# Landmark attention and group norms on one core: five moved or reshaped steps in the second stage, and shorter chains for three norms

## What is computed

```python
x = x + proj(softmax(q.T k) v)           # first stage: group norm (8 groups, weight and bias), 8 heads
u = group_norm(x, 32 groups)             # no weight, no bias
x = x + conv3(dwconvs(u)) * u            # depth-wise convolutions in bands
t = tokens(x)                            # 1024 tokens of 128 channels an image
n = layer_norm(t)                        # second stage
q, k, v = n Wqkv + bqkv                  # 8 heads of 16, landmarks: every 64th token, 16 of them
K1 = softmax(q k_lm.T); K2 = softmax(q_lm k_lm.T); K3 = softmax(q_lm k.T)
z = newton_inverse(K2, 6 steps)          # z = 2 z - z K2 z
t = t + (K1 (z (K3 v))) Wproj + bproj
g = softmax(layer_norm(t) Wg); top 2 of 8 experts, their weights normalised
t = t + sum_e score_e (gelu(n W1_e + b1_e) W2_e + b2_e)
t = t + dense_attention(layer_norm(t))   # third stage
t = t + gated_silu_experts(layer_norm(t))  # top 6 of 16, with two shared experts
```

## Time and profile before

| | us |
|---|---|
| median of 3 runs | 5484.53 |
| lowest and highest run | 5480.68 and 5505.98 |
| the profiled execution | 5477.94 |
| its span in the profile | 5476.1 |
| PE busy | 4820.5 (88%) |
| DVE busy | 3578.8 (65%) |
| ACT busy | 2948.8 (54%) |
| POOL busy | 1017.9 (19%) |
| mean granted clock of PE | 0.953 |

### The profile page before, as it was taken

The page is one execution under the profiler, slowest core; times in us unless marked ns, Lnnn a source line. Parts: engine busy times, 40 slices in busy tenths (PEclk is TensorE's granted clock), DMA queues, the critical chain, the costliest instruction groups (busy, mean ns, idle before and its releaser), DMA issues.

```text
span 5476.1 us, 81744 instructions
## 1 busy us (share of the span) xinstructions
PE 4820.5 (88%) x25601; PEld 2609.5 (48%) x25601; DVE 3578.8 (65%) x7699; ACT 2948.8 (54%) x5390; POOL 1017.9 (19%) x1348
## 2 busy tenths in 40 slices
PE   5888888888888886967999899999899999999999
PEld 1222222222222221335888888888755555555554
DVE  6677777777776772646666666665676766766765
ACT  2555566555655654423555555556655455555552
POOL 2211211121212212211434334343200000000000
PEclk7999999999999998987999999999999999999999
DMA  2522222222222221222555455554311111111112
GB/s 85 147 71 71 76 89 71 71 71 71 71 83 71 72 74 32 30 68 83 154 165 173 140 176 154 164 170 116 109 49 46 52 46 48 51 43 52 51 46 74
DMA packets 406296, 477.08 MB, mean 87 GB/s; under 512 B 87640, under 2 KB 249648, under 8 KB 403760
## 3 DMA queue, kind: packets, MB, share of 16 engines
q1 hardware_dynamic: 372128, 424.84, 25.5%
q0 software_dynamic: 20576, 35.55, 2.4%
q10 hardware_dynamic: 13168, 11.48, 0.8%
HBM read 308.54 MB, written 145.57 MB: 83 GB/s over the span
## 4 chain that ended last, share of the span: by engine, by line
PE 30%; DVE 12%; issue 4%; ACT 4%; DVEq 3%; POOL 2%; DMA 1%; ACTq 0%; SPq 0%; POOLq 0%
PE n_ps_f L2155 4%; PE n_ps_f L2148 4%; PE n_ps_xy L1803 3%; PE n_ps_h L1793 3%; PE n_ps_c L2195 2%; PE n_ps_h L2207 2%; POOL rows_scratch L1313 2%; PE n_ps_f L2142 2%; PE n_ps_f L1654 1%; PE n_ps_xy L2211 1%; PE n_ps_h L2211 1%; DVEq L2027 1%; DVE n_down_weights L2026 1%; PE n_ps_f L995 1%; ACT n_hidden L1609 1%
## 5 line engine op out<-in xcount | busy, mean ns | idle before, releaser
L597 ACT ACTIVATE a_probs<-ps_b 128x512 f32<-128x512 f32 x2048 | 1110.7, 594 | 800.4 <-PE ps_b L693 787.5
L454 DVE TENSOR_REDUCE a_negmax<-ps_a 128x1 f32<-128x1024 f32 x1024 | 1206.4, 1219 | 384.5 <-PE ps_a L637 374.8
L637 PE MATMUL ps_a<-a_k_stack,a_q_stack 96*128 96x512 bf16 x2048 | 635.6, 397 | 181.4 <-DVE a_negmax L454 89.8
L693 PE MATMUL ps_b<-a_q_stack,a_k_stack 99*128 99x512 bf16 x2048 | 675.0, 392 | 67.5 <-ACT a_probs L597 30.6
L1609 ACT ACTIVATE n_hidden<-n_ps_h,n_b 128x128 f32<-128x128 f32 x1472 | 420.4, 374 | 402.6 <-PE n_ps_h L1793 399.1
L706 PE MATMUL ps_o<-a_probs,a_v_ones 128*32 128x512 f32 x4096 | 561.8, 621 | 0.2 <-ACT a_probs L597 0.2
L637 PEld LDWEIGHTS ps_a<-a_k_stack,a_q_stack 96*128 96x128 bf16 x2048 | 146.3, 99 | 736.4 <-DVE a_negmax L454 470.2
L1803 PE MATMUL n_ps_xy<-n_down_weights,n_hidden 128*128 x2944 | 402.6, 280 | 56.1 <-ACT n_hidden L1609 30.2
L693 PEld LDWEIGHTS ps_b<-a_q_stack,a_k_stack 99*128 99x128 bf16 x2048 | 196.7, 100 | 486.4 <-ACT a_probs L597 247.0
L1803 PEld LDWEIGHTS n_ps_xy<-n_down_weights,n_hidden 128*128 128x128 f32 x2944 | 363.4, 193 | 86.7 <-issue 83.1
L2092 ACT ACTIVATE n_down_weights<-n_ps_h 128x512 f32<-128x512 f32 x288 | 172.4, 599 | 427.7 <-PE n_ps_h L2207 318.5
(11 more groups left out here) (350 smaller groups left out, 7485.5 us busy)
## 6 DMA issues: line engine op xcount, KB each, us to landing
n_up_weights<-in_L_ffn_W_dram SPq DMA_DIRECT2D x368, 256.0 KB
n_up_weights<-score_scratch SPq DMA_DIRECT2D x512, 128.0 KB, 2.9
split_scratch<-a_pieces SPq DMA_DIRECT2D x180, 256.0 KB
a_q_stack<-split_scratch SPq DMA_DIRECT2D x128, 192.0 KB, 3.4
a_k_stack<-split_scratch SPq DMA_DIRECT2D x128, 192.0 KB, 4.0
rows_scratch<-n_zero SPq DMA_DIRECT2D x16, 1472.0 KB
outs_scratch<-n_xy SPq DMA_DIRECT2D x176, 128.0 KB
n_xg<-rows_scratch SPq DMA_DIRECT2D x80, 256.0 KB, 4.7
```

Source lines behind the costliest of these rows:

```text
L454: dve.tensor_reduce(negmax[:, b, t:t + 1], bank, axis=AX.X, op=ALU.max, negate=True).then_inc(ring_read, 1)
L597: act.activation(probs[:, m % PROBS, 512 * k:512 * k + 512], ps_b[:, k, :], ACT.Exp).then_inc(b_exp, 1)
L637: last = pe.matmul(bank[:, cols], q_stack[0:KS, h, 128 * t:128 * t + 128], k_stack[0:KS, h, cols], start=True, stop=True)
L693: pe.matmul(ps_b[:, k, :], k_stack[:, h, 128 * t:128 * t + 128], q_stack[:, h, 512 * k:512 * k + 512], start=True, stop=True).then_inc(b_u ...
```

## The change

In the second stage:

- *Landmarks.* `k_lm` is written from the projection's PSUM bank with the bias added in the same instruction, as soon as PE has written it, and not from `kt`. ACT's `kt` (which used to be what the landmarks waited for) now waits for `lm_up`, and PE's K3 product at slot 19 gets a wait for `kt` of its own.
- *Bias.* PE's second bias product moves from slot 36 to 39, DVE's second addition from 38 to 40.
- *Norm.* The choice's layer norm yields to slot 4 at n == 3, one step later.
- *Key weights.* The sums over the landmark weights (L1406) move from behind the first Newton step to ahead of the Newton loop; the reciprocal stays where it was.
- *Exponential.* ACT's exponential of the choice moves from slot 14 to 17, DVE's part of the choice behind it from 16 to 18.

In the norms:

- `rsqrt` has ten instructions instead of eleven: the multiplication by -0.5 goes into the middle instruction of each Newton step.
- `group_affine` becomes `group_scale` with `rsqrt_column`: the variance is formed as minus one half of itself, and each Newton step takes two instructions instead of three, with a column as the scalar operand. The shift is no longer part of it: "norm" forms it in one instruction with weight and bias, "norm2" in one of its own, and the second norm's scale and shift are written where the later stage reads them, without the copies.

```diff
 def rsqrt(dve, y, v, t):
     dve.tensor_scalar(y.bitcast(I32), v.bitcast(I32), -0.5, 1597463007.0, ALU.mult, ALU.add)
-    dve.drain()
-    dve.tensor_scalar(v, v, -0.5, None, ALU.mult)
     for _ in range(3):
         dve.drain()
         dve.tensor_tensor(t, y, y, ALU.mult)
         dve.drain()
-        dve.tensor_tensor(t, t, v, ALU.mult)
+        dve.scalar_tensor_tensor(t, t, -0.5, v, ALU.mult, ALU.mult)
...
+def rsqrt_column(dve, out, y, minus_half, t):
+    dve.tensor_scalar(y.bitcast(I32), minus_half.bitcast(I32), -0.5, 519526879.0, ALU.mult, ALU.add)
+    dve.drain()
+    for n in range(3):
+        dve.scalar_tensor_tensor(t, y, minus_half, y, ALU.mult, ALU.mult)
+        dve.drain()
+        dve.scalar_tensor_tensor(out if n == 2 else y, t, 1.5, y, ALU.add, ALU.mult)
+        dve.drain()
...
-def group_affine(dve, scale, shift, group, sums, sums_read, width, small, eps):
+def group_scale(dve, scale, group, sums, sums_read, width, small, eps):
...
-    dve.tensor_tensor(small[:, 0:1], group[:, 0:1], group[:, 0:1], ALU.mult)
+    dve.scalar_tensor_tensor(small[:, 0:1], group[:, 0:1], 0.5, group[:, 0:1], ALU.mult, ALU.mult)
...
-    dve.tensor_tensor(small[:, 1:2], group[:, 1:2], small[:, 0:1], ALU.subtract)
+    dve.scalar_tensor_tensor(small[:, 1:2], group[:, 1:2], -0.5, small[:, 0:1], ALU.mult, ALU.add)
...
-    dve.tensor_scalar(small[:, 1:2], small[:, 1:2], 0.0, eps, ALU.max, ALU.add)
+    dve.tensor_scalar(small[:, 1:2], small[:, 1:2], 0.0, -0.5 * eps, ALU.min, ALU.add)
...
-    rsqrt(dve, scale, small[:, 1:2], small[:, 2:3])
-    dve.scalar_tensor_tensor(shift, group[:, 0:1], -1.0, scale, ALU.mult, ALU.mult)
-    dve.drain()
+    rsqrt_column(dve, scale, small[:, 0:1], small[:, 1:2], small[:, 2:3])
...
                 elif what == "norm2":
-                    dve.tensor_copy(gn2[:, 0, bass.ds(prev, 1)], gscale[:, :])
-                    dve.tensor_copy(gn2[:, 1, bass.ds(prev, 1)], gshift[:, :])
-                    dve.tensor_scalar(xn[:, :], x1[:, :], gscale[:, :], gshift[:, :], ALU.mult, ALU.add)
+                    scale, shift = gn2[:, 0, prev:prev + 1], gn2[:, 1, prev:prev + 1]
+                    dve.scalar_tensor_tensor(shift, group[:, 0:1], -1.0, scale, ALU.mult, ALU.mult)
+                    dve.drain()
+                    dve.tensor_scalar(xn[:, :], x1[:, :], scale, shift, ALU.mult, ALU.add)
...
                 elif what == "norm":
                     dve.tensor_tensor(gscale[:, :], gscale[:, :], nw[:, :], ALU.mult)
-                    dve.tensor_tensor(gshift[:, :], gshift[:, :], nw[:, :], ALU.mult)
                     dve.drain()
-                    dve.tensor_tensor(gshift[:, :], gshift[:, :], nb[:, :], ALU.add)
+                    dve.scalar_tensor_tensor(gshift[:, :], group[:, 0:1], gscale[:, :], nb[:, :], ALU.mult, ALU.subtract)
                     dve.drain()
...
-                for src, dst, up in ((qt, q_lm, 1), (kt, k_lm, 2)):
-                    dve.wait_ge(S["qk_up"], i * 2 + up)
...
-                last.then_inc(S["lm_up"], 1)
+                dve.wait_ge(S["qk_up"], i * 2 + 1)
+                dve.tensor_tensor(by_head(q_lm), b16, every(qt), ALU.mult)
+                dve.wait_ge(S["qk_ps"], i * 2 + 2)
+                dve.scalar_tensor_tensor(by_head(k_lm), every(pa), kb[:, :], b16, ALU.add, ALU.mult).then_inc(S["lm_up"], 1)
...
                 dve.tensor_scalar(zt[:, :], m2[:, :], fro[:, :], None, ALU.mult).then_inc(S["z0_up"], 1)
+                dve.wait_ge(S["k1_exp"], i + 1)
+                dve.tensor_reduce(sum1[:, :], k1v, axis=AX.X, op=ALU.add)
+                dve.drain()
                 for it in range(NEWTON):
...
                     if it == 0:
-                        dve.wait_ge(S["k1_exp"], i + 1)
-                        dve.tensor_reduce(sum1[:, :], k1v, axis=AX.X, op=ALU.add)
-                        dve.drain()
                         dve.reciprocal(sum1[:, :], sum1[:, :])
...
                 for n, last in enumerate(token_norm_steps(dve, xln2, tok, stats2, mv2, var2, inv2, tmp2)):
-                    if n == 2:
+                    if n == 3:
                         yield 4
...
-                yield 16
+                yield 18
                 dve.wait_ge(S["exp_up"], i + 1)
-                yield from spread(16, gate_choose_steps(dve, gate, E, K, 1e-6, tie[:, :]))
+                yield from spread(18, gate_choose_steps(dve, gate, E, K, 1e-6, tie[:, :]))
...
                 for k in range(HALVES):
-                    yield 36 + 2 * k
+                    yield 36 + 4 * k
                     dve.wait_ge(S["b2_ps"], i * HALVES + k + 1)
...
                 act.wait_ge(S["qk_ps"], i * 2 + 2)
+                act.wait_ge(S["lm_up"], i + 1)
                 act.activation(kt[:, :], pa[:, :], ACT.Identity, bias=kb[:, :]).then_inc(S["qk_up"], 1)
...
-                yield 14
+                yield 17
                 act.wait_ge(S["shift_up"], i + 1)
...
                 yield 19
+                pe.wait_ge(S["qk_up"], i * 2 + 2)
                 wide(pa, q_lm[:, :], kt).then_inc(S["s3_ps"], 1)
...
                 for k in range(HALVES):
-                    yield 34 + 2 * k
+                    yield 34 + 5 * k
                     if k:
                         pe.wait_ge(S["base_up"], i * HALVES + 1)
```

More of the change, by code:

```diff
@@ L477, in step @@
                     width, eps = ((C // 8, 1e-5), (C // 32, 1e-5))[work[1]]
-                    group_affine(dve, gscale[:, :], gshift[:, :], group, bank[:, 0:2], ring_read, width, small, eps)
+                    scale = gn2[:, 0, prev:prev + 1] if work[1] else gscale[:, :]
+                    group_scale(dve, scale, group, bank[:, 0:2], ring_read, width, small, eps)
                 elif what == "norm2":
-                    dve.tensor_copy(gn2[:, 0, bass.ds(prev, 1)], gscale[:, :])
-                    dve.tensor_copy(gn2[:, 1, bass.ds(prev, 1)], gshift[:, :])
-                    dve.tensor_scalar(xn[:, :], x1[:, :], gscale[:, :], gshift[:, :], ALU.mult, ALU.add)
+                    scale, shift = gn2[:, 0, prev:prev + 1], gn2[:, 1, prev:prev + 1]
+                    dve.scalar_tensor_tensor(shift, group[:, 0:1], -1.0, scale, ALU.mult, ALU.mult)
+                    dve.drain()
+                    dve.tensor_scalar(xn[:, :], x1[:, :], scale, shift, ALU.mult, ALU.add)
                     dve.drain()
@@ L491, in step @@
                     dve.tensor_tensor(gscale[:, :], gscale[:, :], nw[:, :], ALU.mult)
-                    dve.tensor_tensor(gshift[:, :], gshift[:, :], nw[:, :], ALU.mult)
                     dve.drain()
-                    dve.tensor_tensor(gshift[:, :], gshift[:, :], nb[:, :], ALU.add)
+                    dve.scalar_tensor_tensor(gshift[:, :], group[:, 0:1], gscale[:, :], nb[:, :], ALU.mult, ALU.subtract)
                     dve.drain()
-                    dve.tensor_scalar(xn[:, :], xf[:, :], gscale[:, :], gshift[:, :], ALU.mult, ALU.add).then_inc(xn_up, 1)
+                    dve.tensor_scalar(xn[:, :], xf[:, :], gscale[:, :], gshift[:, :], ALU.mult, ALU.subtract).then_inc(xn_up, 1)
                     dve.drain().then_inc(xf_free, 1)
@@ L1342, in front @@
                 yield 17
-                for src, dst, up in ((qt, q_lm, 1), (kt, k_lm, 2)):
-                    dve.wait_ge(S["qk_up"], i * 2 + up)
-                    last = dve.tensor_tensor(dst[:, :].rearrange("p (h l) -> p h l", h=HEADS), b16,
-                                             src[:, 0:N:STEP].unsqueeze(1).broadcast_to((128, HEADS, LM)), ALU.mult)
-                last.then_inc(S["lm_up"], 1)
+                every = lambda ap: ap[:, 0:N:STEP].unsqueeze(1).broadcast_to((128, HEADS, LM))
+                by_head = lambda ap: ap[:, :].rearrange("p (h l) -> p h l", h=HEADS)
+                dve.wait_ge(S["qk_up"], i * 2 + 1)
+                dve.tensor_tensor(by_head(q_lm), b16, every(qt), ALU.mult)
+                dve.wait_ge(S["qk_ps"], i * 2 + 2)
+                dve.scalar_tensor_tensor(by_head(k_lm), every(pa), kb[:, :], b16, ALU.add, ALU.mult).then_inc(S["lm_up"], 1)
                 yield 19
```

## The result

The changed kernel takes **5434.15 us** (median of 4 runs, 5414.35 to 5435.98) where the kernel before takes 5491.98 (4 runs): ratio 0.9885, 95% interval 0.985 to 0.992. Measured again on another chip it was 5427.56 (5 runs), ratio 0.9880 (0.9859 to 0.9901). That is 58 us less, faster by over 0.5%. The forecast was 5453 us, and its range of 5410 to 5482 holds the result; but it expected 31.5 us of gain, little more than half, and the result lies just outside the 5437 to 5468 that it gave to its own case.

What follows compares the result with a forecast made beforehand. PE, busy 84%, 90% and 93% of the stages, was taken as the bound through its waits; gains of 11 + 3 + 11 + 6.5 = 31.5 us off the runs' median 5484.53 gave 5453 us, range 5410 to 5482.

Steps and rivals of the forecast that it cites:

- its own case: Whole kernel: the forecast's summed gains hold, giving 5453 us within 5437 to 5468; chance 0.39.
- first stage 11: First stage: shorter group-norm chains give 8.6 us over the images, plus 1.2 and 1.1 bare; 11 us (5 to 14).
- rounds 11: Second stage's fourteen rounds: each gains 1.1 + 0.4 - 0.7 = 0.8 us, 11 us in all (-13 to 45).
- lead-in 3: Two images worked on ahead of the second stage's ring: gain the kt and part of the sum, 3 us (0 to 5).
- third stage 6.5: Dense stage: two shorter rsqrt chains in each of 14 rounds, 28 x 0.245 = 6.5 us (3 to 7).
- PE 0.6 earlier: Second half of a round, choice's norm: PE's 1.2 us wait goes, ACT gives back half; 0.6 us (0 to 1.2).
- that leaves 0.4 to 1.1 an image, I take 0.7: First stage: PE's shorter wait for the first norm's score reduction gains 0.7 us an image, 8.6 in all.
- The clock's price in the rounds: First half of a round: PE's longer wait for scatter and load brings low clock, costing 0.7 us a round.
- 1.1 + 0.4: A round's gains: indices 1.1 us earlier from the second half, 0.4 us from the moved bias product in the first.
- DVE runs on until the first Newton copy: Second half of a round: 2.4 us of displaced choice work follows L1354, so DVE works unbroken until that copy.
- The rival of the late exponential: Second stage: a late exponential delays each round and makes the kernel slower, 20 us lost, 5505 us; chance 0.08.
- The 1.3 that "could" be earlier: Second half of a round: landmark scores could start 1.3 us earlier with keys read from the projection's bank.

Runs made afterwards that it cites:

- undo_exp: The changed kernel with ACT's exponential of the choice back at slot 14 and DVE's part behind it at 16; 5410.10 us, ratio 0.9848.
- undo_land: The changed kernel with landmark keys read from the moved keys again and the keys' move without its wait; 5423.22 us, ratio 0.9877.
- v_late: The changed kernel with DVE's addition of the value bias moved behind the first Newton step; 5429.66 us, ratio 0.9879.

## Why the prediction was right, and where it was not

The sum came out with the right sign and short by nearly half, so that the result is in the range and outside the forecast's own part of it: first stage 11, rounds 11, lead-in 3, third stage 6.5 were predicted; measured over the profiles: about 29 (2070.3 in two kernels without these norms, 2041.3 in eleven with them), 23.7, nothing (451.8 us from the last maximum to the first indices for 451.3) and 7.2, less 2.8 in the last round. Together 57. Most of what is missing are two terms of the clock: some 15 us in the first stage that were left out, and 10 in the rounds that were taken off. Both erred the same way. Two products of the working are off by little: 0.7 in twelve images is 8.4 and not 8.6, and 28 x 0.245 is 6.9 and not 6.5. The norm's "PE 0.6 earlier" is worked out but is no term of the sum.

- **First stage.** The step "that leaves 0.4 to 1.1 an image, I take 0.7" was right for the wait, and the term was mis-sized, because it had only the wait. PE's idle time fell by 14.1 us (291.8 in the two without, 277.7 in the eleven with), its busy time by 14.9 (1778.5 to 1763.6). The prediction priced the clock behind a wait that grows, in the second stage, and not behind one that shrinks, although the low stretches at the norms stood in the same trace. The Trainium skill's "TensorE: Matmul & The Clock Gate", section "HAM oscillation", tells of a loop that waits for a transfer in every turn and starts each at the low clock. The rows agree for this loop, which waits for DVE as well as for transfers, with a stretch at 10 to 14 of the sixteen norms.
- **The clock's price in the rounds, 0.7 each, 10 in all.** This step failed: it had the stretches that come and not those that go. They came as forecast: behind PE's first rows seven, nine and seven stretches of low clock begin in the fourteen rounds of the three kernels with the five steps, and one, three and two in those without. But behind the second bias product, whose wait the change removes, it is none with the steps and eight, seven and eight without. (At the waits ahead of the first Newton products there are more with the steps, ten or eleven for five to seven.) Here is one of each kind, in the changed kernel behind its wait of 3.69 us for the rows, and in the kernel before behind a wait of 1.36 us for the first addition:

```profile
2860.00:2864.00 4.00, 2.82 (x13) 2.59 (x14) 2.99 (x22) 0.60 (x1) 0.00 (x0) 0.62 0.85 233
```
```profile
2961.03 1.15 PE L1768 MATMUL n_ps_c<-n_b,n_score_t 8*128 8x128 f32 x8 [1.36 <-DVE maps L1518]
```
```profile
2963.00:2966.00 3.00, 3.00 (x16) 3.00 (x16) 0.00 (x0) 0.60 (x1) 2.22 (x3) 0.50 0.21 65
```

  In all, half of PE's busy time at low clock went from 37.7 to 38.6 us, 0.1 a round for 0.7. This is most of what is missing in the rounds: 1.1 + 0.4 without the price is 21 us, and 23.7 were measured.
- **The two halves.** From the indices to PE's first rows a round takes 26.1 us for 26.8, so 0.7 were gained there for the 0.4 taken. From the first rows to the indices it is 58.2 for 58.7 in this pair of profiles, and 58.1 for 59.0 in the means of three kernels with the five steps and three without: 0.9 for the 1.1 foreseen.
- **Key weights.** The times came out as foreseen: in the mean of three kernels each, the first copy stayed (48.5 us behind PE's first rows for 48.3; 15.3 behind the exponential's end, 15.2 foreseen), and the second came 0.9 earlier, 3.1 us behind the first for 4.1 before. But this step is not what gained it: undone (undo_keys), the first copy comes 1.0 sooner behind the exponential and the second 1.1 later behind the first.
- **Exponential.** "DVE runs on until the first Newton copy" describes what the trace shows, and "L1354 starts only some 0.35 us earlier" is nearly so: 34.4 us behind PE's first rows for 34.5 in the means of three kernels each, where undo_exp has 33.2. The price was missed. That the unbroken run passes L1386, on which PE waits at L1701, was not looked at. The step gives back more than the gelus' 20 us. The rival of the late exponential was thus partly true: the step costs some 17 us against the kernel without it, 13 of them in the rounds and the last round, hidden under the others. The table load itself is as in the earlier trace rows, 1.28 us with the exponential 1.30 behind its start. The Trainium skill's "ScalarE: Activation LUTs", section "What ACT_TABLE_LOAD costs", adds a drain to each load. It does not show in these 1.30 us.
- **Landmarks.** The wait went. The 1.3 that "could" be earlier was left as an upper bound: rightly with this exponential; with the early one the step is worth 20 us, 13 of them in the rounds.
- **Norm and bias.** Both waits went and both came back elsewhere: the bias's at the load (24.4 us), as the step said, the norm's at ACT (6.0). In idle time the bias is worth 3.8 (5.6 foreseen) and the norm 1.5 (8, if its 0.6 a round had been counted); neither is clear of chance.
- **Third stage.** 7.2 for 6.5: right.

Of what was to be seen: L1677, L1768 and L1738 left PE's waits, the compares stand right ahead of the maximum, the rows' load is waited for 1.0 to 3.7 us in each round. L1354 is 0.1 earlier and not a few tenths, L663's wait is 6.4 and not below 5, and the indices are 0.5 us earlier in this pair of profiles, 0.9 in the means, for 1.1.

## What to carry to other kernels

When a wait of PE is shortened or lengthened, look also at the granted clock right behind it, in both directions: here half of a stage's gain was faster matmuls, not less waiting, and in the rounds the low stretches behind a new wait stood against those that left with an old one. Compare PE's idle and busy time separately over the same instructions, and take means over the rounds and over several profiles: one round read alone can be the slowest. And when several repairs go in together, undo each in the finished kernel: one of these five cost some 17 us, and it was the one that made another (20 us) worthless.

## What the runs showed of the hardware that was not expected

The long and the short low-clock stretch behind nearly equal waits, above. And a gap on POOL: in two of the fourteen rounds, the same two in the kernel before, the changed one, undo_exp, undo_land and v_late, the second scatter follows the first after a pause of 2.2 us in which POOL waits for nothing that the profile shows; elsewhere it is 0.3.

```profile
2833.04 0.99 POOL L1321 DMA_INDIRECT rows_scratch<-n_xln,n_index_out  x1 [30.69 <-DVE n_index_out L1474]
2836.24 0.97 POOL L1321 DMA_INDIRECT rows_scratch<-n_xln,n_index_out  x1 [2.21 <-issue]
2837.52 0.96 POOL L1321 DMA_INDIRECT rows_scratch<-n_xln,n_index_out  x1 [0.30 <-issue]
```

In the changed kernel the whole pause lands on PE: those two rounds have the waits of 3.7 us for the rows, the others 1.0 to 2.0. Its cause was not tried.
